# Second pass of a whitening kernel: all of it in 64x128 tiles, the transposed image stationary

## The reference

```
x = x + _L0_conv_ref(_gn(x), L0_conv_weight_re, L0_conv_weight_im, L0_conv_bias)
x = x + _L1_conv_ref(_gn(x))

# _L1_conv_ref, x seen as (b, w, h, c): c is the last axis of the image
x_flat = jnp.transpose(x, (3, 0, 1, 2)).reshape(c, -1)
f = x_flat - mean
fg = f.reshape(groups, M_PER_GROUP, -1)
cov = jnp.einsum('gmn,gkn->gmk', fg, fg) / denom
...
inv_sqrt = jax.vmap(lambda L: jax.scipy.linalg.solve_triangular(L, eye, lower=True))(chol)
f_hat = jnp.einsum('gmk,gkn->gmn', inv_sqrt, fg)
```

## Time and profile before

| | |
|---|---|
| median of 3 runs | 3541.8 us |
| profiled execution, its own time | 3536.93 us |
| its span (first to last instruction) | 3535.0 us |
| TensorE busy in the span | 2898.4 us, 82% |
| VectorE busy | 2541.8 us, 72% |
| ScalarE busy | 1146.3 us, 32% |
| GpSimd busy | 1116.4 us, 32% |
| moved by DMA | 1001.81 MB, 283 GB/s over the span |

### The profile page before, as it was taken

The page is one execution under the profiler, slowest core; times in us unless marked ns, Lnnn a source line. Parts: engine busy times, 40 slices in busy tenths (PEclk is TensorE's granted clock), DMA queues, the critical chain, the costliest instruction groups (busy, mean ns, idle before and its releaser), DMA issues.

```text
span 3535.0 us, 230090 instructions
## 1 busy us (share of the span) xinstructions
PE 2898.4 (82%) x98565; PEld 2038.3 (58%) x98565; DVE 2541.8 (72%) x4358; ACT 1146.3 (32%) x2860; POOL 1116.4 (32%) x1434
## 2 busy tenths in 40 slices
PE   6888888888886342366499999999999999999998
PEld 3555555555554332122377777777777777777776
DVE  4777777777776335755477777777777777777777
ACT  1222222222221221000144444444444444444444
POOL 4666666666665112455111111111111111111111
PEclk8999999999998555799799999999999999999999
DMA  7999999999999761699388888888888888888887
GB/s 229 330 322 331 327 330 323 326 326 327 333 327 274 93 92 19 205 349 352 118 302 302 302 300 301 301 302 300 301 302 301 302 303 300 301 302 302 300 300 279
DMA packets 630257, 1001.81 MB, mean 283 GB/s; under 512 B 103712, under 2 KB 464176, under 8 KB 630192
## 3 DMA queue, kind: packets, MB, share of 16 engines
q1 hardware_dynamic: 528816, 912.44, 78.5%
q10 hardware_dynamic: 101376, 88.39, 8.7%
HBM read 639.40 MB, written 361.28 MB: 283 GB/s over the span
## 4 chain that ended last, share of the span: by engine, by line
PE 50%; issue 15%; ACT 14%; ACTq 10%; DMA 6%; DVE 5%; SPq 0%; DVEq 0%; POOL 0%; POOLq 0%
PE bank L593 15%; ACT reg L645 13%; PE bank L584 11%; ACTq L653 6%; PE bank L421 6%; DMA reg<-xh_d 5%; PE bank L432 5%; PE bank L440 4%; PE bank L454 3%; PE bank L564 2%; PE bank L501 2%; PE bank L525 1%; ACT xh L645 1%; DVE reg L866 1%; PE bank L463 1%
## 5 line engine op out<-in xcount | busy, mean ns | idle before, releaser
L645 ACT ACTIVATE reg<-bank 128x512 f32<-128x512 f32 (+3 forms) x1696 | 844.7, 529 | 1105.7 <-PE bank L593 941.1
L1064 DVE STREAM_TRANSPOSE reg<-bank 128x256 f32<-128x256 f32 x2048 | 738.8, 418 | 335.5 <-PE bank L610 335.5
L768 POOL TENSOR_TENSOR reg<-reg 128x512 f32<-128x512 f32 x512 | 685.9, 1340 | 433.8 <-PE bank L432 402.0
L1068 DVE SCALAR_TENSOR_TENSOR reg<-reg,m,mwhit 128x1024 f32<-128x1024 f32 x512 | 657.8, 1285 | 72.1 <-DVE reg L1064 38.2
L593 PE MATMUL bank<-tab,reg 64*128 64x256 f32 x4096 | 692.5, 404 | 0.0
L822 POOL TENSOR_TENSOR reg<-reg,tab 128x64 f32<-128x64 f32 x512 | 164.2, 321 | 1550.1 <-ACT reg L645 828.0
L854 DVE TENSOR_TENSOR reg<-reg 128x512 f32<-128x512 f32 x512 | 526.5, 1028 | 36.6 <-DVE gmask L872 20.2
L610 PE MATMUL bank<-reg 32*32 32x128 f32 x32768 | 547.0, 279 | 1.7 <-DVE reg L1064 1.7
L610 PEld LDWEIGHTS bank<-reg 32*32 32x32 f32 x32768 | 370.5, 103 | 210.3 <-issue 171.5
L584 PE MATMUL bank<-tab,reg 64*128 64x64 f32 x8704 | 443.5, 235 | 46.2 <-ACT reg L645 46.1
L593 PEld LDWEIGHTS bank<-tab,reg 64*128 64x128 f32 x4096 | 458.5, 187 | 28.0 <-issue 0.7
(11 more groups left out here) (121 smaller groups left out, 1765.2 us busy)
## 6 DMA issues: line engine op xcount, KB each, us to landing
reg<-in_x_dram SPq DMA_DIRECT2D x256, 1024.0 KB, 8.2
reg<-in_x_dram SPq DMA_DIRECT2D x512, 512.0 KB, 3.9
out_dram<-reg SPq DMA_DIRECT2D x512, 512.0 KB, 2.9
xh_d<-xh ACTq DMA_DIRECT2D x128, 512.0 KB
reg<-xh_d SPq DMA_DIRECT2D x128, 512.0 KB, 5.9
gram_d<-gram ACTq DMA_DIRECT2D x64, 256.0 KB
reg<-gram_d SPq DMA_DIRECT2D x64, 256.0 KB, 4.8
spec_d<-psu ACTq DMA_DIRECT2D x512, 8.5 KB
```

Source lines behind the costliest of these rows:

```text
L645: copy = lambda o, i, **k: nc.scalar.activation(o, i, ACT.Copy, **k)
L768: nc.gpsimd.tensor_tensor(out=halves[:, q % 2, 1], in0=x_in[:, 2 * q:2 * q + 2, 0], in1=x_in[:, 2 * q:2 * q + 2, 1], op=ALU.subtract).then ...
L1064: ins = v.transpose(o_sb[:, q].rearrange("p n (f w) -> p f n w", f=2)[:, :, :, BL * j:BL * j + BL], bank[4 + j][:, 0:W].rearrange("p (f n ...
L1068: v.scalar_tensor_tensor(out=o_sb[:, q], in0=o_sb[:, q], scalar=m1[:, ds(t * 4 + q, 1)], in1=mwhit[:, :].unsqueeze(1).to_broadcast([P, 4, W]),
```

## The change

The whitening's operands swap places. The turned image is now stationary, in 64x128 pieces (64 columns of the image by two channels of 64 rows, which `xt_sb` now keeps side by side), and a 64x64 piece of the whitening matrix moves. The result therefore comes out with the rows on the partitions, as the store needs it, and VectorE's four transposes go; its final operation reads the accumulators, in two halves. Whitening is 16 products of 64 columns instead of 32 of 128, and uses two sets of two banks, in turn. The turn of the spectrum becomes two 64x64 products. ScalarE copies bank 2, VectorE (`turned_image`) bank 3. The factors `wr`, `wp` and `wd` double in width (64 instead of 32), with an identity of 64 columns in the table. The turn of the spectrum moves behind the whitening, and the waits of `may_whiten` to its head.

```diff
     put("eye32", np.tile(np.eye(BL), (P // BL, 2)))
+    put("eye64", np.tile(np.eye(KH), (2, 1)))
...
-        xt_sb, a = cut(big, a, 2, 2, 2, H)
-        wr, a = cut(big, a, 2, 2, BL)
-        wp, a = cut(big, a, 2, 2, BL)
-        wd, a = cut(big, a, 2, BL)
+        xt_sb, a = cut(big, a, 2, 2, 4, P)
+        wr, a = cut(big, a, 2, 2, KH)
+        wp, a = cut(big, a, 2, 2, KH)
+        wd, a = cut(big, a, 2, KH)
         cs, a = cut(big, a, 2, 2, KH)
+        mwhit, a = cut(big, a, 4, W)
...
                 pe.wait_ge(*nth("z_ready", t * 2 + m))
-                mm(bank[0][:, W:W + P], cs[:, m].rearrange("p a b -> p (a b)"), T("eye"), start=True, stop=True,
-                   is_transpose=True).then_inc(S["ct_mm"], 1)
+                for c in range(2):
+                    k = slice(KH * c, KH * c + KH)
+                    ins = mm(bank[c][:, W:W + KH], cs[k, m].rearrange("p a b -> p (a b)"), T("eye")[k, k],
+                             start=True, stop=True, is_transpose=c == 1)
+                ins.then_inc(S["ct_mm"], 1)
...
-            def turn(t, q, before=None):
+            def turn(t, q):
 
                 pe.wait_ge(*nth(f"x_re_in{q}", t * 16 + 16))
-                pe.wait_ge(*nth("xt2_copied", t * 8 + 2 * q))
+                pe.wait_ge(*nth("xt2_act", t * 4 + q))
+                pe.wait_ge(*nth("xt2_dve", t * 4 + q))
...
-                pe.wait_ge(*nth("z_ready", t * 2 + q // 2 + 1))
-                for half in range(2):
-                    for c in range(2):
-                        k = slice(KH * c, KH * c + KH)
-                        if half == 1 and c == 1 and before is not None:
-                            may_whiten(*before)
-                        ins = mm(bank[2 + c][:, H * half:H * half + H], z_sb[k, q // 2, q % 2, P * half:P * half + P],
-                                 T("hb")[k], start=False, stop=True, skip_group_check=True)
-                        if half == 1:
-                            ins.then_inc(S["xt2_mm"], 1)
-
-            def may_whiten(t, q):
-
-                pe.wait_ge(*nth("w_ready", t * 4 + q + 1))
-                pe.wait_ge(*nth("xt2_copied", t * 8 + 2 * q + 2))
-                pe.wait_ge(*nth("o_turned", t * 4 + q))
-
-            def whitened(t, q):
+
+            def convolved(t, q, half):
+
+                if half == 0:
+                    pe.wait_ge(*nth("z_ready", t * 2 + q // 2 + 1))
+                for c in range(2):
+                    k = slice(KH * c, KH * c + KH)
+                    ins = mm(bank[2 + c][:, H * half:H * half + H], z_sb[k, q // 2, q % 2, P * half:P * half + P],
+                             T("hb")[k], start=False, stop=True, skip_group_check=True)
+                    if half == 1:
+                        ins.then_inc(S["xt2_mm"], 1)
+
+            def whitened(t, q, part):
+
                 e = q % 2
-                for half in range(2):
-                    for i in range(4):
-                        for j in range(4):
-                            r = slice(BL * j, BL * j + BL)
-                            ins = mm(bank[4 + j][BL * i:BL * i + BL, P * half:P * half + P],
-                                     wp[r, e, half], xt_sb[r, e, half, i // 2].rearrange(
-                                         "p (n h) -> p n h", h=KH)[:, :, BL * (i % 2):BL * (i % 2) + BL],
-                                     start=half == 0, stop=True, skip_group_check=True)
-                ins.then_inc(S["o_mm"], 1)
+                if part == 0:
+                    pe.wait_ge(*nth("w_ready", t * 4 + q + 1))
+                    pe.wait_ge(*nth("xt2_act", t * 4 + q + 1))
+                    pe.wait_ge(*nth("xt2_dve", t * 4 + q + 1))
+                    pe.wait_ge(*nth("o_ready", t * 4 + q - 1))
+                for r in ((0,), (1,), (2, 3))[part]:
+                    for half in range(2):
+                        for g in range(2):
+                            k = slice(KH * g, KH * g + KH)
+                            at = P * r + KH * half
+                            ins = mm(bank[4 + 2 * e + g][:, at:at + KH], xt_sb[k, e, half, r], wp[k, e, half],
+                                     start=r == 0 and half == 0, stop=True, skip_group_check=True)
+                if part == 2:
+                    ins.then_inc(S["o_mm"], 1)
 
             def four(t, first=False, last=False):
 
                 for q in range(4):
                     before = (t, q - 1) if q >= 1 else (t - 1, 3) if not first else None
                     ahead = (t, 1) if q < 2 else (t + 1, 0) if not last else None
-                    if q % 2 == 0 and ahead:
-                        spectrum_turned(*ahead)
-                    turn(t, q, before)
+                    turn(t, q)
+                    for half in range(2):
+                        convolved(t, q, half)
                     if q % 2 == 1 and ahead:
                         widened(*ahead)
                     if before:
-                        whitened(*before)
+                        for part in range(3):
+                            whitened(*before, part)
+                    if q % 2 == 0 and ahead:
+                        spectrum_turned(*ahead)
...
-            copy(mwhit[:, :], bank[4][:, 0:W], scale=1.0 / ROWS).then_inc(S["mw_ready"], 1)
-            for j in range(4):
-                r = slice(BL * j, BL * j + BL)
-                ins = copy(wd[r], whit[r, :, BL * j:BL * j + BL])
+            for r in range(4):
+                ins = copy(mwhit[:, r], bank[4][:, 0:W], scale=1.0 / ROWS)
+            ins.then_inc(S["mw_ready"], 1)
+            for g in range(2):
+                k = slice(KH * g, KH * g + KH)
+                ins = copy(wd[k], whit[k, :, KH * g:KH * g + KH])
...
                     act.wait_ge(*nth("o_mm", t * 4 + q - 1))
-                    for c in range(2):
-                        act.wait_ge(*nth("xt2_mm", t * 8 + 2 * q + c + 1))
-                        copy(xt_sb[:, q % 2, :, c], bank[2 + c][:, :].rearrange("p (f h) -> p f h", f=2)
-                             ).then_inc(S["xt2_copied"], 1)
+                    act.wait_ge(*nth("xt2_mm", t * 8 + 2 * q + 1))
+                    copy(xt_sb[:, q % 2, :, :, 0:KH], bank[2][:, :].rearrange("p (f r h) -> p f r h", f=2, r=4)
+                         ).then_inc(S["xt2_act"], 1)
+                    if q % 2 == 1 and not (last and q >= 2):
+                        widened_kept(*((t, 1) if q < 2 else (t + 1, 0)))
...
-                                            in1=T("eye32").rearrange("p (a b) -> p a b", a=2),
+                                            in1=T("eye64").unsqueeze(1).to_broadcast([P, 2, KH]),
...
+            def turned_image(t, q):
+
+                dve.wait_ge(*nth("o_mm", t * 4 + q - 1))
+                dve.wait_ge(*nth("xt2_mm", t * 8 + 2 * q + 2))
+                v.tensor_copy(xt_sb[:, q % 2, :, :, KH:P], bank[3][:, :].rearrange("p (f r h) -> p f r h", f=2, r=4)
+                              ).then_inc(S["xt2_dve"], 1)
+
             def result(t, q):
                 dve.wait_ge(*nth(f"out_stored{q}", t * 16))
                 dve.wait_ge(*nth("o_mm", t * 4 + q + 1))
-                for j in range(4):
-                    ins = v.transpose(o_sb[:, q].rearrange("p n (f w) -> p f n w", f=2)[:, :, :, BL * j:BL * j + BL],
-                                      bank[4 + j][:, 0:W].rearrange("p (f n h) -> p f n h", f=2, n=4))
-                ins.then_inc(S["o_turned"], 1)
-                dve.wait_ge(*nth("o_turned", t * 4 + q + 1))
-                v.scalar_tensor_tensor(out=o_sb[:, q], in0=o_sb[:, q], scalar=m1[:, ds(t * 4 + q, 1)],
-                                       in1=mwhit[:, :].unsqueeze(1).to_broadcast([P, 4, W]),
-                                       op0=ALU.add, op1=ALU.subtract).then_inc(S["o_ready"], 1)
+                for g in range(2):
+                    by = lambda a: a.rearrange("p r (f g w) -> p (r f) g w", f=2, g=2)[:, :, g]
+                    ins = v.scalar_tensor_tensor(
+                        out=by(o_sb[:, q]), in0=bank[4 + 2 * (q % 2) + g][:, :].rearrange("p (n w) -> p n w", n=8),
+                        scalar=m1[:, ds(t * 4 + q, 1)], in1=by(mwhit), op0=ALU.add, op1=ALU.subtract)
+                ins.then_inc(S["o_ready"], 1)
 
             def four(t, first=False):
                 for q in range(4):
+                    turned_image(t, q)
```

More of the change, by code:

```diff
@@ L36 @@
 NI = KX // 2
-COLS = dict(hc=KH, wj=2 * KW, hb=H, e0=W, e1=W, rot=P, fold=KW + 1, eye=P, eye32=2 * BL, dc=1, hk=1, hh=1,
+COLS = dict(hc=KH, wj=2 * KW, hb=H, e0=W, e1=W, rot=P, fold=KW + 1, eye=P, eye32=2 * BL, eye64=KH, dc=1, hk=1, hh=1,
             sgn=1, dcrow=1, pick=PAIRS, ones=P, mean=P)
@@ L226, in whiten_kernel @@
         fac = sb("fac", [M, M])
-        whit, msum, mwhit = sb("whit", [P, 2, P]), sb("msum", [P, 2, P]), sb("mwhit", [P, W])
+        whit, msum = sb("whit", [P, 2, P]), sb("msum", [P, 2, P])
         o_sb, a = cut(reg1, 0, 4, 4, W) if NP >= 256 else cut(sb("o_buf", [P, 4096]), 0, 4, 4, W)
```

(30 more changed lines are left out.)

## The result

The changed kernel takes 3616.7 us (median of four runs, 3606.6 to 3630.3) against 3540.9 us for the one before in the same runs: a ratio of 1.0215, 95% interval 1.0178 to 1.0252. It is slower, by 76 us, and the interval lies on both sides of 2%; 3675 was forecast, 3560 to 3785 the range. The profiled execution took 3620.3 us with a span of 3618.5.

A forecast was written before the change was run, and what follows sets the result against it. TensorE's work plus hand-over stalls was taken to bound the stage. Per double pair 2 x (1.63 + 1.79) + 0.43 + 0.22 = 7.49 us against 6.96, +136 us on 3537: 3673, given as 3675; range 3560 to 3785.

The forecast's parts named there:

- What bounds and what goes: Second pass over the image: TensorE's work plus hand-over stalls bounds it; line 610's passes, shape changes and waits go.
- The whitening's price: New whitening on TensorE: 16 passes per tile, each bound by its stationary load, 0.112 us a pass, 1.79 us a pair.
- What stays: TensorE from a pair's first transpose to the end of the addition's last pass: 1.63 us a pair.
- The expansion: TensorE's two expansion products, two passes each on each of the two row tiles: 0.43 us per double pair.
- the spectrum's turn: On TensorE, a plain 64x64 product and a transposed one: 0.22 us per double pair, its own 0.49 us stall gone.
- The signs: Expected profile: whitening block 1.75 to 1.85 us, loads about 185 ns, pairs 3.6 to 3.9 us, DMA about 280 GB/s.
- The copy's 0.69 us: VectorE's one copy of 128x512 from the accumulators per pair, priced at 0.69 us.
- VectorE's two additions: VectorE's two additions of 512 columns from the accumulators per pair, priced at 1.3 to 1.4 us.
- B: Whitening loads hide as in the transposes, 0.0615 us a pass; DMA then binds at 3.1 us a pair, about 3350; chance 0.12.
- C: In-between case for the whitening: passes of 0.08 to 0.10 us, 3500 to 3590 us; chance 0.07.
- D: Whitening: load and stream of a tile don't overlap, 0.165 us a pass, about 4110 us; chance 0.04.
- E: Whitening passes start strictly in program order, so tiles wait for each other: 0.125 us a pass, about 3780 us; chance 0.05.

The follow-up runs named there:

- e1: The changed kernel with 96 instead of 128 stationary columns in each whitening product, part of the whitening left out; 3408.6 us.
- e2: The changed kernel with 32 instead of 64 moving columns in each whitening product, half of the whitened columns left out; 3609.3 us.
- e8: The changed kernel without the whitening itself: its products turn the image back in transpose form, but for the first on each tile; 3149.8 us.
- e5: The kernel before, with the spectrum's turn in its new form and place and the whitening's waits moved directly ahead of the whitening; 3349.1 us, ratio 0.9484.
- e7: The kernel before, with only the whitening's waits moved directly ahead of the whitening and the old turn of the spectrum; 3532.9 us, ratio 0.9988.
- e4: The kernel before, with only the spectrum's turn changed to two 64x64 products behind the even pair's whitening; 3521.0 us, ratio 0.9967.
- e3: The changed kernel with 8 whitening products of 128 moving columns instead of 16 of 64, half of the image's columns left out; 3181.6 us.

## Why the prediction was right, and where it was off

*What bounds and what goes*: right. TensorE's own work is the stage, its stalls are gone, and VectorE, ScalarE and GpSimd have room. The slowdown itself was oversized: +136 us forecast, +83.5 in the profiled spans and +76 in the medians.

*The whitening's price*: the mechanism is shown (e1, e2, e8), and the size was right. The passes of a tile follow each other at 0.112 us, the value taken, so 16 of them are 1.79 us. The chain says 1.74, as it divides at the ends of matmuls and so books 0.05 us of each whitening with the next pair's transposes.

*What stays*, forecast at 1.63 us from a pair's start to the end of the addition, is the mis-sized term. On the row tile that has more to do, the trace has two plain passes at 0.112, seven transposes at 0.062 and four passes of the addition at 0.216 us, 1.52 us. (The chain, by its division, says 0.60 + 0.975 = 1.58.) I had read the term from pairs that began with TensorE idle. There the first plain load lies open ahead of the first matmul, whose record contains it; in a stream without stalls that load runs under the last matmuls of the whitening. The first matmul of a pair is recorded with 0.32 us before, where a plain one in the stream has 0.27 and a transpose 0.22:

```profile
2503.46 0.32 PE L584 MATMUL bank<-tab,reg 64*128 64x64 f32 x1
```

The expansion (0.42 against 0.43) and the spectrum's turn (0.24 against 0.22) were right.

Together, on that tile: 2 x (1.52 + 1.79) + 0.43 + 0.22 = 7.27 us for two pairs instead of 7.49; the measured period is 7.28. The 0.21 us between 7.49 and 7.28, times 256, are 54 us, and 3673 - 54 = 3619 against 3620 for the profiled execution.

*The signs*: the loads (188 ns), the stage's clock (1.00), DMA (287 GB/s) and VectorE's wait (681 us over 512 pairs, 1.33 each) came as said. The whitening's block is 1.69 us from first to last start and not 1.75 to 1.85, because the first interval on a tile is short (the second matmul is recorded from before its load is done, 0.27 us against 0.22 for the first); the pairs are 3.39 and 3.89 us and not all between 3.6 and 3.9, because the expansion falls into every second one.

*Smaller slips*: "99% busy in every slice" is more than a digit 9 says (90% or more); the window has 1669 of 1780 us, 94%. The copy's 0.69 us came out (692 ns) partly by luck, as line 1068 gives 1.25 ns a column and not 1.0. VectorE's two additions take 1.41 us a pair (721.8 us over 512), at the upper end of the estimate.

*The rivals*: B is refuted by the changed kernel's own passes, and e8 shows that the fast rate belongs to the transpose form. B's floor was also wrong, 2.76 us a pair (e8) and not 3.1, so with short loads TensorE's 2.93 us a pair would have been the bound, about 3255 us and not 3350. C's range doesn't follow from its passes: by the prediction's own sum 0.10 us a pass gives about 3580 us, but 0.08 gives about 3415 and not 3500. C, D and E fall with the pass of 0.112. E's premise can be read in the earlier trace rows after all: a pass of line 593 starts at 4.05, ahead of the last one of line 584 at 4.10, which stands before it in the program. So across the two row tiles, starts do not follow the program's order, and this trace does not bear out the rule that the prediction names beside E.

*Where the change's good side went*: it removes the stalls of 0.33 and 0.49 us at shape changes and those for ScalarE's copies, and its whitening takes 1.74 us of the chain in every pair where line 610's 64 passes took 1.07. Of the 0.49 us ahead of line 564 the change of shape is not all: e5 has 0.20 us at its change from 32x32 to 64x128 tiles, and in e7 the stall grew to 0.80, for ScalarE's copy. e5 also shows that the waits for ScalarE could be had without the new whitening, by moving the waits and by moving the spectrum's turn in its new form.

## What to carry to other kernels

Where operands swap places, count the stationary columns loaded per unit of time, not the multiplications: 64x128 tiles with 64 moving columns in plain float32 are bound by their loads, and halving the moving columns changed nothing beyond the spread of the runs (e2) while a quarter fewer stationary columns took 200 us off (e1 against e2). Before an operation is rebuilt to get rid of stalls, try to move the waits and the small operations around it; and where two chains wait in parallel, remove both at once, since each alone may show nothing (e4, e7, e5). A term that is read from a stretch behind a stall contains the stall's start-up, here 0.1 us a pair.

## What the hardware showed unexpectedly

The same 64x128 float32 operand loads in 188 ns in a plain product and in 139 ns in a transpose, and passes follow each other at 0.112 against 0.062 us. DMA's share of 0.85 at 300 GB/s in the kernel before was no sign of a floor near 3.0 us: the same transfers ran at 372 and 380 GB/s (e3, e8) once TensorE let them.
